# Another order of the work in the last four slots of layer 0

## The reference

```
h = layernorm(x) * (1 + ca) + sa
x = x + ga * attn(h)
h = layernorm(x) * (1 + cb) + sb
x = x + gb * (h @ (wscale * sign(weight) + wbias).T)

attn: per head and chunk of 128 tokens
  scores  = q k^T                         decay = exp(G_i - G_j), causal
  y       = (scores * decay) @ xc + (q * exp(G)) @ state
  state   = state * exp(G_last) + (k * exp(G_last - G))^T @ xc
  y       = y / rms(y) * gnorm_w * silu(gate)
  out     = y @ Wo^T
```

## Time and profile before

| What | Value |
|---|---|
| median of 3 runs | 1512.79 us (1510.37 to 1515.64) |
| profiled execution, its own time | 1508.06 us |
| its span | 1506.3 us |
| granted TensorE clock, mean over the span | 0.915 |
| busy: PE, DVE, ACT, POOL | 1240.5, 1007.1, 622.7, 732.3 us |

### The profile page before, as it was taken

The page is one execution under the profiler, slowest core; times in us unless marked ns, Lnnn a source line. Parts: engine busy times, 40 slices in busy tenths (PEclk is TensorE's granted clock), DMA queues, the critical chain, the costliest instruction groups (busy, mean ns, idle before and its releaser), DMA issues. The chain is left out here.

```text
span 1506.3 us, 18429 instructions
## 1 busy us (share of the span) xinstructions
PE 1240.5 (82%) x6008; PEld 876.0 (58%) x6008; DVE 1007.1 (67%) x1721; ACT 622.7 (41%) x1166; POOL 732.3 (49%) x740
## 2 busy tenths in 40 slices
PE   4889999999999999999999999876989998961000
PEld 2678767767776777777777777655753333430000
DVE  6746665565655566655655656666678888748898
ACT  2334333333433433334434433334517777753203
POOL 0456765656655756656656665675420012031107
PEclk9999999999999999999999999998979999985555
DMA  4211122122123121121221211130185310000001
GB/s 161 81 50 56 57 69 86 43 77 71 56 58 91 49 71 48 58 78 42 64 70 50 63 50 64 57 99 1 37 181 93 48 58 2 2 1 0 1 0 56
DMA packets 70488, 86.47 MB, mean 57 GB/s; under 512 B 6789, under 2 KB 40741, under 8 KB 69818
## 3 DMA queue, kind: packets, MB, share of 16 engines
q1 hardware_dynamic: 68138, 81.52, 19.6%
q10 hardware_dynamic: 2256, 3.77, 0.9%
HBM read 77.49 MB, written 7.51 MB: 56 GB/s over the span
## 5 line engine op out<-in xcount | busy, mean ns | idle before, releaser
L1473 ACT ACTIVATE yTh<-yF 128x512 fp32r<-128x512 f32 x64 | 40.4, 631 | 318.9 <-DVE yF L1045 318.9
L1692 POOL TENSOR_TENSOR sw<-sw,sinT 128x512 f32<-128x512 f32 x80 | 103.4, 1293 | 138.5 <-ACT sw L1424 138.5
L1207 DVE TENSOR_REDUCE nm<-banks 128x2 f32<-128x1024 f32 x128 | 151.2, 1218 | 25.8 <-PE banks L752 25.7
L1706 POOL TENSOR_TENSOR dec<-gb,gcol 128x512 f32<-128x512 f32 x64 | 70.6, 1104 | 195.4 <-DVE Sd L1011 191.3
L1584 ACT ACTIVATE Pb<-banks 128x512 f32<-128x512 f32 x256 | 135.0, 601 | 47.6 <-PE banks L773 47.3
L983 DVE SCALAR_TENSOR_TENSOR gs<-tg,banks 128x512 f32<-128x512 f32 x64 | 44.0, 687 | 118.6 <-ACT tg L1431 118.6
L547 PE MATMUL banks<-hTh,wgh 128*128 128x512 f32 x256 | 122.1, 477 | 0.0
L599 PE MATMUL banks<-st,qt 128*128 128x128 f32 x384 | 80.4, 293 | 37.1 <-DVE Sd L1011 21.1
L627 PE MATMUL banks<-woh,yTh 128*128 128x512 f32 x256 | 104.9, 410 | 3.5 <-DVE yTl L1048 3.5
L547 PE MATMUL banks<-hTh,wqh 128*128 128x512 f32 x256 | 106.3, 415 | 0.0
L627 PE MATMUL banks<-woh,yTl 128*128 128x512 f32 x256 | 101.5, 397 | 0.0
(11 more groups left out here) (310 smaller groups left out, 3269.3 us busy)
## 6 DMA issues: line engine op xcount, KB each, us to landing
gb<-g_scr SPq DMA_DIRECT2D x64, 256.0 KB, 3.4
raw<-in_wmod SPq DMA_DIRECT2D x40, 256.0 KB, 2.7
raw<-in_wg SPq DMA_DIRECT2D x32, 256.0 KB, 2.7
raw<-in_wo SPq DMA_DIRECT2D x32, 256.0 KB, 2.8
raw<-in_wq SPq DMA_DIRECT2D x30, 256.0 KB, 2.7
qsT<-q_scr SPq DMA_DIRECT2D x22, 256.0 KB, 6.9
q_scr<-hl SPq DMA_DIRECT2D x28, 128.0 KB, 4.6
mt<-mods_scr SPq DMA_DIRECT2D x12, 256.0 KB, 4.7
```

The costliest lines, as they stand in the source:

```text
L1207: ve.tensor_reduce(nm[:, b, i, p:32:16], pairs[z_][:, :].rearrange("p (g t) -> p g t", g=2), AX.X, ALU.max, negate=True).then_inc(*v_nm.up ...
L1692: po.tensor_tensor(s_[:, :], s_[:, :], sinT[:, :], ALU.mult).then_inc(*g_rope.up("sin", kind, t, n))
L1706: po.tensor_tensor(dec[:, :, :], gb[s % 2][:, :, :], bc(gcol[:, t % 2, heads(t), n], 2, 128), ALU.subtract).then_inc(*g_dec.up("sub", s))
```

## The change

`last_slot` calls its steps in another order. The gate and product steps of a slot come first, `state` stands ahead of `norm_pow` and `norm_b`, `fold_b` ahead of the loads, and after them come `prep(s + 2)` and `prep_exp(s + 2)` (before: those of s + 1 at the slot's start) and `beside_outputs`, which stood ahead of `outputs`. `prep` and `prep_exp` of slot 61 are called once ahead of the four slots. The two sign steps `w_values(1)` and `w_values(2)` move from the end of slot 59 to the end of slot 60, and of the four `w_turn` two are in slot 60 and two in slot 61 (before: three and one). No instruction is added or removed.

```diff
--- before.py
+++ after.py
@@ -2157,12 +2157,13 @@
     def beside_outputs(E, s):
 
         if s == NSLOT - 4:
+            E.w_values(1), E.w_values(2), E.w_values(3)
             E.tables(0, None), E.tables(1, None)
-            E.w_values(3)
-            for k in range(3):
+            for k in range(2):
                 E.w_turn(k, E.bank())
         elif s == NSLOT - 3:
-            E.w_turn(3, E.bank())
+            for k in range(2, 4):
+                E.w_turn(k, E.bank())
             E.col_turn(E.bank())
             E.residual("f", 0), E.residual("f", 1)
         elif s == NSLOT - 2:
@@ -2175,27 +2176,25 @@
     def last_slot(E, s):
 
         ahead = s + 1 < NSLOT
-        if ahead:
-            E.prep(s + 1)
         E.fold_a(s - 1)
-        if ahead:
-            E.prep_exp(s + 1)
-        beside_outputs(E, s)
         E.outputs(s)
         E.norm_a(s)
         if ahead:
+            E.prep2(s + 1, ("xc",))
             E.scores(s + 1)
-            E.prep2(s + 1, ("xc",))
+        E.state(s)
         E.norm_pow(s)
+        E.norm_b(s)
+        if ahead:
+            E.prep2(s + 1, ("qt", "xd"))
+        E.fold_b(s - 1)
         if s + 2 < NSLOT:
             E.load_gb(s + 2)
         if ahead:
             E.start_loads(s - NSLOT + 5)
-        E.norm_b(s)
-        E.state(s)
-        if ahead:
-            E.prep2(s + 1, ("qt", "xd"))
-        E.fold_b(s - 1)
+        if s + 2 < NSLOT:
+            E.prep(s + 2), E.prep_exp(s + 2)
+        beside_outputs(E, s)
 
     def turn(E, of, b, k, bk):
         E.turn_h(of, b, k, bk, *E.spare((of, b, k)))
@@ -2503,9 +2502,8 @@
                 E.split()
             if s == NSLOT - 6:
                 E.w_values(0)
-            if s == NSLOT - 5:
-                E.w_values(1), E.w_values(2)
         E.scores(NSLOT - 4)
+        E.prep(NSLOT - 3), E.prep_exp(NSLOT - 3)
         for s in range(NSLOT - 4, NSLOT):
             last_slot(E, s)
         last_folds(E)
```

## The result

The changed kernel takes 1520.65 us (median of 13 runs, 1516.48 to 1526.00), the kernel before 1511.82 us in the same comparison (13 runs). The ratio is 1.0058 (95% interval 1.0043 to 1.0073), so 8.8 us slower (6.5 to 11.0). A second comparison of the two gave 1.0052 (1.0033 to 1.0072). The direction I forecast holds. The size, +3.8 us, was less than half of it. The time lies near the upper end of the range.

A forecast was written before the change was run, and what follows sets the result against it. No engine is full; a chain of hand-overs between engines bounds the kernel. Steps through slots 60 to 63 put tile 3's moments at 1013.8 against 1010.01, so 1512.8 + 3.8 = 1516.6 us, range 1508.5 to 1521.5.

The forecast's parts named there:

- The weight's term: Slot 60: VectorE's signs 2.27 plus 0.8 lost beside GpSimd, then scalings 1.90, before TensorE turns the weight.
- Three terms: TensorE in slots 60 to 62: turns and outputs 4.96, slot 61's products 4.45, slot 62's at full pace 2.97.
- the mark: Start of tile 3's moments on VectorE, 1010.01 before, forecast 1013.8; the end moves by as much, +3.8 us.
- slot 62's term: Slot 62's products with Wo at full pace, 2.97 us; +1.5 in the upper bounds if slow too.
- The turns of `hh`: After tile 3's moments, first at 1012.96 before; what follows hangs on them link by link, with no new place.
- What is won elsewhere ends in nothing: Slot 63's `yn` and slot 62's addition come some 3 to 5 us earlier, but only steps needing `hh` wait behind.
- Rival A: GpSimd and VectorE hold each other up at every moved step, slots 60 to 62: 1519.5 us; chance 0.17.
- the ring: Each slot's circle of hand-overs between engines; slot 60's 2 us won was to be spent on the weight's 5 us.
- B: No effect: TensorE keeps its pace through the gaps, lower bound within 1.5 us, 1512.8 us; chance 0.16.
- C: Faster: the end follows slot 63's own work, not the moments, 1508 us; chance 0.12.
- the forecast's +5.5: Upper end of the forecast's band for the whole kernel, +1.5 to +5.5 us, given chance 0.55.
- the sum of all upper bounds: Whole change at +6.7 us, with signs losing 2.2 (+1.4) and slot 62's products slow too (+1.5).

The follow-up runs named there:

- moments-ahead run: Changed kernel with `beside_outputs` of slot 63 back ahead of its outputs and norm; ratio to before 1.0015.
- signs in the gap: Changed kernel with `prep_exp(s + 2)` behind the other work, slot 63's moments ahead again, the two signs between slot 60's `yF` and `yTl`; ratios to before 0.9979, 0.9988.
- both: Changed kernel with `prep_exp(s + 2)` behind the other work of slots 60 to 62 and slot 63's moments ahead of its outputs again; ratio to before 0.9984.
- moments behind: Kernel before, with only slot 63's moments of tiles 1 to 3 moved behind its norm and slot 62's addition; ratio to before 1.0032.
- exponentials behind: Changed kernel with `prep_exp(s + 2)` moved behind the other work of slots 60 to 62; ratio to before 1.0024.

## Why the prediction was right in direction and too small

By its own steps, all counted from the addition that opens slot 60:

| Step | Predicted | First profile | Second |
|---|---|---|---|
| slot 59's products with Wo start | 6.0 | 6.0 | 6.0 |
| addition of slot 59 | 9.0 | 9.1 | 9.1 |
| turns of the weight | 14.6 | 15.4 | 15.4 |
| slot 61's outputs end | 19.5 | 20.0 | 21.3 |
| decay of slot 63 | 26.0 | 26.5 | 27.3 |
| last two `fTh` | 28.9 | 29.4 | 30.3 |
| slot 61's products with Wo | 34.6 | 35.4 | 36.3 |
| addition of slot 61 | 39.0 | 40.1 | 41.8 |
| addition of slot 62 | 47.1 | 49.9 | 50.0 |
| tile 3's moments | 49.8 | 52.6 | 52.7 |

- **The waits were right**, each of them: `yTh` behind two exponentials, TensorE 6.31 us idle before the turns, `fTh` behind slot 63's transfer, moments behind slot 62's addition. The experiments show the last two by undoing them.
- **The weight's term was 0.7 us short.** I gave the signs and scalings 2.27 + 0.8 + 1.90 = 5.0; from the signs' start to the turns it was 5.66. The signs lost 1.12 beside GpSimd (3.47 against 2.35), not 0.8, and the scalings 0.2. GpSimd lost more than that, 1.8 us on the two decay steps of slot 62 (before: 1.05 and 0.63):

```profile
976.20 2.03 POOL L1706 TENSOR_TENSOR dec<-gb,gcol 128x512 f32<-128x512 f32 x1
978.38 1.43 POOL L1708 TENSOR_SCALAR_AFFINE_SELECT dec<-dec 128x512 f32<-128x512 f32 x1
```

Taken apart, the two signs ran from 975.84 to 977.32 and from 977.25 to 979.31, 1.48 and 2.06 us against 1.22 each before. GpSimd's `xdd` ended at 976.24, its first decay step at 978.23, 0.91 us behind the first sign's end, and the second sign 1.08 behind that. The two engines took turns, each instruction held up by the one of the other engine that was under way. That agrees with the Trainium skill, page "SBUF — State Buffer", section "Who interferes with whom", by which a VectorE instruction with two SBUF inputs and a GpSimd instruction that reads SBUF contend for a port pair that only one of them can hold. What doesn't follow from it is my reading of it, one whole GpSimd instruction of loss for each sign (2.1 us): the first sign met only the end of one. Slot 61's `yTl`, 1.54 against 0.69 beside a residual addition, lost 0.85 us in the same way, where I had 0.4.
- **The step that was sized too small is the pace of TensorE behind its idle times.** Three terms hold it: 4.96 for the turns and slot 61's outputs, 4.45 for slot 61's products, and in slot 62 "1.44 + 0.75 to TensorE, which was busy with the tables and slot 63's outputs, so 2.97 at full pace". Together 12.4 us; measured 4.68 + 4.70 + 4.66 = 14.0 in the first profile and 5.98 + 5.53 + 3.07 = 14.6 in the second. In the first profile it is the last term that failed: the products took 4.63 us in the chain, with a granted clock of 0.51 over 3.3 us of them, 1.7 us of the missing 2.8 at the mark. TensorE had been busy for 8 us, but at half clock for the first 3.5, and then idle for 2.00 us. In the second profile that term was right and the other two were 1.0 and 1.1 us short. I had a row for a gap of 3.5 us and none for 2 or 5, and took one outcome for each; my upper bound had held slot 62's term at +1.5.
- **The turns of `hh` behind the mark** I took as rigid. They follow 5.72 us of idling and started slow: 0.5 us.
- "What is won elsewhere ends in nothing" was right: slot 63's `yn` came 2.2 us earlier, not 3 to 5, and nobody waited for it. Slot 62's addition, forecast as early as that too, came no earlier than before (49.9 both). Rival A's place was right and its price not: VectorE's losses beside GpSimd came to about 2 us on the ring, of which I had counted 1.2. B falls with the clock rows, C with the moments-ahead run.
- With the products of slot 62 at the slow price the sum is 3.8 + 1.7 = 5.5 us, past the 4.5 that a measurement tells from nothing; I held "no change that can be told" for likelier than "slower".
- **That the time lies within the range is in part luck.** The measured 8.8 us is past the forecast's +5.5 and past the sum of all upper bounds, 6.7; the range reached to +8.7 by room left for rival A, and not for TensorE's pace. It was counted from 1512.8, and the kernel before measured 1511.8 in the comparison.

## What to carry to other kernels

A step put at the end of a stage waits for everything that stands ahead of it on its engine, not for what it reads; before moving "other work" behind a stage, look what it feeds and whether the stage's last wait was the gap that it filled. On an engine in order, an instruction that waits for a transfer is harmless only if nothing of the current stage stands behind it. Where a change opens idle time ahead of TensorE's products, price them at half clock from a row that shows it. For gaps near 2 us reckon with either outcome, since here the same kernel gave both, and take a second profile before you lay a loss at one place.

## What the runs showed of the hardware

- Behind 5.2 and 5.6 us of idling TensorE's granted clock was 0.50, for 3.5 us in one profile of the changed kernel and for all of slot 61's products in the other: they took 4.68 and 5.50 us. Filled with additional products, the gap left the clock at 1.00. A gap of 1.52 us in slot 60 (972.14) left the products behind it at full pace.
- Near 2 us both outcomes occur. Behind gaps of 1.85 us (signs in the gap, first profile), 1.95 (changed, second profile), 1.99 (both) and 2.24 (moments behind) twelve products started within 2.7 us; behind 2.00 (changed, first profile), 2.05 (signs in the gap, second profile) and 2.16 (exponentials behind) within 4.2. No limit can be read from these rows.
- Two 128 x 1024 instructions of VectorE with two inputs in SBUF took 2.35 us beside an idle GpSimd and 3.47 us beside a busy one, which itself lost 1.0 and 0.8 us on two instructions. The lengths fit turns: each waited for the instruction that the other engine had under way.
- Layer 1's maxima took 203.1 to 206.8 us in four executions of two kernels that are the same there, so a single span cannot tell a change of 4 us; a mark counted from a nearby start repeated within 0.1 to 1.7 us.
